# Two Mixtures of Experts on One Core: logits three beats ahead, gates two, and a beat of TensorE in two equal halves

## The reference

```python
router_probs = jax.nn.softmax(x @ router_w + router_b, axis=-1)
top_p, top_i = jax.lax.top_k(router_probs, K)
top_p = top_p / jnp.sum(top_p, axis=-1, keepdims=True)
expert_out = jnp.einsum('bnd,edc->bnec', x, expert_w) + expert_b
gathered = jnp.take_along_axis(expert_out, top_i[..., None], axis=2)
return jnp.einsum('bnk,bnkc->bnc', top_p, gathered)
```

## Time and profile before

| what | value |
|---|---|
| three runs, us | 6378.89, 6384.5, 6384.5 |
| the profiled execution, us | 6384.87 |
| its span, us | 6383.1 |
| mean granted TensorE clock | 0.899 of full speed |
| busy over the span: TensorE, VectorE, ScalarE, POOL | 80%, 68%, 54%, 18% |
| DMA: bytes moved, GB/s over the span | 646.31 MB, 101 |

### The profile page before, as it was taken

How to read it: one execution, slowest core, us unless ns; L and a number is a source line. 1 busy time by engine, 2 the same in 40 slices (tenths; PEclk the granted TensorE clock), 3 DMA queues, 4 the chain that set the end, 5 groups by cost and what they waited for, 6 DMA issues and landing times. The chain is left out here.

```text
span 6383.1 us, 130752 instructions
## 1 busy us (share of the span) xinstructions
PE 5087.2 (80%) x47166; PEld 3307.8 (52%) x47166; DVE 4320.6 (68%) x9480; ACT 3439.0 (54%) x6809; POOL 1148.8 (18%) x1068
## 2 busy tenths in 40 slices
PE   7887887449968885799969997109999999758887
PEld 4664663224523332799969994105555555423332
DVE  7896987696757777522233447697777777568886
ACT  5665665475545664422243226267777767545553
POOL 2332332162200003300000000231121111211110
PEclk9998998759979996799989999559999999878998
DMA  1111113232358884100000235146666666357776
GB/s 36 35 31 35 38 35 92 60 105 90 106 177 275 277 283 141 56 0 0 0 0 0 79 105 146 53 103 77 84 84 84 84 81 81 53 164 236 231 221 213
DMA packets 745076, 646.31 MB, mean 101 GB/s; under 512 B 496551, under 2 KB 578663, under 8 KB 744627
## 3 DMA queue, kind: packets, MB, share of 16 engines
q1 hardware_dynamic: 734387, 634.86, 40.1%
q10 hardware_dynamic: 9216, 4.20, 0.2%
q0 software_dynamic: 1024, 1.05, 0.1%
HBM read 549.78 MB, written 90.20 MB: 100 GB/s over the span
## 5 line engine op out<-in xcount | busy, mean ns | idle before, releaser
L2444 PE MATMUL sw_pC<-sw_row,sw_wc 128*128 128x128 f32 x10160 | 1158.6, 274 | 56.2 <-DVE sw_row L2319 55.0
L2444 PEld LDWEIGHTS sw_pC<-sw_row,sw_wc 128*128 128x128 f32 x10160 | 1147.4, 191 | 58.2 <-DVE sw_row L2319 55.5
L2878 PE MATMUL sp_pC<-sp_work,sp_bands 64*64 64x512 f32 (+11 forms) x14592 | 985.5, 428 | 43.4 <-issue 43.4
L2307 DVE SCALAR_TENSOR_TENSOR sw_row<-sw_pC,sw_y 128x128 f32<-128x128 f32 x1016 | 338.2, 333 | 790.9 <-PE sw_pC L2444 790.9
L2878 PEld LDWEIGHTS sp_pC<-sp_work,sp_bands 64*64 64x64 f32 x14592 | 600.4, 133 | 431.8 <-issue 363.8
L2817 ACT ACTIVATE sp_pC<-sp_pC,sp_par 128x512 f32<-128x512 f32 x832 | 598.4, 741 | 369.3 <-PE sp_pC L2878 346.6
L2015 PE MATMUL t_pO<-t_z,t_ew 128*64 128x512 f32 x2048 | 584.4, 689 | 251.2 <-DVE t_z L1824 235.0
L1824 DVE TENSOR_TENSOR t_z<-t_z,t_ht 128x1024 f32<-128x1024 f32 x512 | 605.1, 1222 | 88.9 <-DMA t_z<-gate_rows 87.4
L2376 ACT ACTIVATE sw_y<-sw_row 128x128 f32 (+1 forms) x762 | 265.9, 349 | 591.8 <-DVE sw_row L2307 591.8
L2774 DVE TENSOR_TENSOR sp_work<-sp_work,sp_pC 128x512 f32<-128x512 f32 x512 | 351.4, 688 | 168.6 <-ACT sp_pC L2817 168.1
L2015 PEld LDWEIGHTS t_pO<-t_z,t_ew 128*64 128x64 f32 x2048 | 132.6, 149 | 553.2 <-issue 267.4
(11 more groups left out here) (385 smaller groups left out, 9576.8 us busy)
## 6 DMA issues: line engine op xcount, KB each, us to landing
t_z<-gate_rows SPq DMA_DIRECT2D x512, 512.0 KB, 6.9
sp_bands<-windows SPq DMA_DIRECT2D x128, 512.0 KB
c_spent<-tokens SPq DMA_DIRECT2D x128, 256.0 KB, 2.6
cb_xs<-tokens SPq DMA_DIRECT2D x128, 256.0 KB, 2.8
wa_xs<-in_x SPq DMA_DIRECT2D x64, 256.0 KB, 2.9
tokens<-wa_xt SPq DMA_DIRECT2D x128, 128.0 KB, 1.9
tokens<-cb_h SPq DMA_DIRECT2D x64, 256.0 KB, 2.7
t_xs<-tokens SPq DMA_DIRECT2D x32, 512.0 KB, 9.5
```

The lines of the kernel that those rows point to most:

```text
L2307: dve.scalar_tensor_tensor(row[par][c][:, :, PAD:PAD + P2], pC[c][:, 0:2 * P2].rearrange("p (b w) -> p b w", b=2), 0.0, line(sweep, c, i), ...
L2444: ins = pe.matmul(pC[c][:, 0:2 * P2], wc[:, sweep, m, :], row[1 - par][c][:, :, m:m + P2], start=(m == 0), stop=(m == 4))
L2878: ins = pe.matmul(out[halves[to], :, low * lo:low * hi], band[halves[k], (NV * g + j) % BANDS, q, AT[k][tap], :], v[halves[k], :, low * at ...
```

## The change

The carried stage gets seven tile buffers instead of six and loads one beat further ahead. The logits are made three beats ahead (TensorE's and ScalarE's m is now n+3) and the gates two (gate, turn_gates and save_gates for n+2). TensorE's beat becomes two halves of like content: mix of a half, turn, add_rest, logits and turn_logits. VectorE's route(n+2) moves from the end of the beat to between the two halves of the first weighing, norm(n+4) to just ahead of it, gate behind the weighing of half 0, stats to the end of the beat and one beat further. ScalarE's root moves to the head of its beat, gap to right behind save_mixed(n, 0), normalise is split over the beat and runs one beat further ahead. A third beat is prepared ahead of the loop.

```diff
--- before.py
+++ after.py
@@ -1571,7 +1571,7 @@
     NB = B * S // (2 * TILE)
     EPS = 1e-5
     BIG = 1e30
-    XR = 6
+    XR = 7
     HR = 3
     with ExitStack() as ctx:
         a = Arena(nc, ctx, stage)
@@ -1657,7 +1657,7 @@
         def x_of(m, i):
 
             if rows is None:
-                return xs[:, m.k, i, :, :]
+                return xs[:, m.n % XR, i, :, :]
             return rows.rearrange("p c b w -> p (b w) c")[:, bass.ds(m.n * J + TS * i, TS), :]
 
         def y_of(m, i):
@@ -1726,8 +1726,8 @@
                     load_columns(2 * n + 11)
                 if n + 1 < NB:
                     spread_gates(n + 1, 0)
-                if rows is None and XR <= n + 4 < NB:
-                    load(n + 4)
+                if rows is None and XR <= n + 5 < NB:
+                    load(n + 5)
                 if n > 0:
                     store(n - 1)
                 if rows is not None and 2 * n + 12 < 2 * NB:
@@ -1821,20 +1821,21 @@
                 dve.wait_ge(ht_saved, 4 * m.n + 2 * i + 2)
                 for q in pairs:
                     dve.wait_ge(g_in[i][q], 16 * m.n + 16)
-                    dve.tensor_tensor(z[:, i, q, :], z[:, i, q, :], ht[:, m.k % HR, i, :], ALU.mult).then_inc(z_ready, 1)
+                    dve.tensor_tensor(z[:, i, q, :], z[:, i, q, :], ht[:, m.n % HR, i, :], ALU.mult).then_inc(z_ready, 1)
 
             def beat(n):
+                later = n.plus(2)
                 weigh(n, 0, [0, 1])
-                if n.plus(1).within(NB):
-                    gate(n.plus(1))
-                weigh(n, 0, [2, 3])
-                if carried is None and n.plus(4).within(NB):
-                    stats(n.plus(4))
-                weigh(n, 1, range(4))
-                if n.plus(2).within(NB):
-                    route(n.plus(2))
                 if carried is None and n.plus(4).within(NB):
                     norm(n.plus(4))
+                if later.within(NB):
+                    route(later)
+                weigh(n, 0, [2, 3])
+                if later.within(NB):
+                    gate(later)
+                weigh(n, 1, range(4))
+                if carried is None and n.plus(5).within(NB):
+                    stats(n.plus(5))
 
             first = Beat(0, 0, 0)
             if carried is None:
@@ -1851,6 +1852,9 @@
             route(first.plus(1))
             if carried is None:
                 norm(first.plus(3))
+            gate(first.plus(1))
+            if carried is None:
+                stats(first.plus(4))
             over_beats(dve, beat)
 
         @block.scalar
@@ -1870,7 +1874,7 @@
                     act.wait_ge(scale_ready, m.n + 1)
                     scale, shift = (v[:, m.k % 2, TS * i:TS * i + TS] for v in (sd, nm))
                 else:
-                    act.wait_ge(x_in[m.k], m.q * 16 + 16)
+                    act.wait_ge(x_in[m.n % XR], 16 * (m.n // XR) + 16)
                     scale, shift = (carried[:, k, J * m.n + TS * i:J * m.n + TS * i + TS] for k in range(2))
                 since(act, h_turned, 4 * m.n + 2 * i - 2)
                 x = x_of(m, i)
@@ -1883,7 +1887,7 @@
                 since(act, z_ready, 8 * m.n - 24 + 4 * i + 4)
                 for s in range(2):
                     act.wait_ge(h_turned, 4 * m.n + 2 * i + s + 1)
-                    act.activation(ht[:, m.k % HR, i, 512 * s:512 * s + 512], pT[s][:, :], ACT.Copy).then_inc(ht_saved, 1)
+                    act.activation(ht[:, m.n % HR, i, 512 * s:512 * s + 512], pT[s][:, :], ACT.Copy).then_inc(ht_saved, 1)
 
             def save_logits(m, i):
                 act.wait_ge(logits_ready, 2 * m.n + i + 1)
@@ -1916,31 +1920,33 @@
                                ACT.Copy).then_inc(y_ready, 1)
 
             def beat(n):
-                m = n.plus(2)
+                m = n.plus(3)
                 due = m.within(NB)
-                ahead = m.plus(1)
-                if n.plus(1).within(NB):
-                    save_gates(n.plus(1))
+                ahead = n.plus(4)
+                later = n.plus(2)
+                if carried is None and ahead.within(NB):
+                    root(ahead)
                 if due:
                     save_turned(m, 0)
                 save_mixed(n, 0)
+                if later.within(NB):
+                    gap(later)
                 if n.n > 0:
                     finish(n.plus(-1), 1)
                 if due:
+                    save_logits(m, 0)
+                if ahead.within(NB):
+                    normalise(ahead, 0)
+                if later.within(NB):
+                    save_gates(later)
+                if due:
                     save_turned(m, 1)
+                save_mixed(n, 1)
                 finish(n, 0)
                 if due:
-                    for i in range(2):
-                        save_logits(m, i)
-                if ahead.within(NB):
-                    normalise(ahead, 0)
-                if carried is None and ahead.plus(1).within(NB):
-                    root(ahead.plus(1))
+                    save_logits(m, 1)
                 if ahead.within(NB):
                     normalise(ahead, 1)
-                if due:
-                    gap(m)
-                save_mixed(n, 1)
 
             def prepare(m, gates_of=None):
                 for i in range(2):
@@ -1960,11 +1966,12 @@
                 root(first.plus(2))
             gap(first)
             prepare(first.plus(1), first)
-            for i in range(2):
-                normalise(first.plus(2), i)
-            gap(first.plus(1))
             if carried is None:
                 root(first.plus(3))
+            gap(first.plus(1))
+            prepare(first.plus(2), first.plus(1))
+            for i in range(2):
+                normalise(first.plus(3), i)
             over_beats(act, beat)
             finish(Beat(NB - 1, (NB - 1) % 6, (NB - 1) // 6), 1)
 
@@ -1977,8 +1984,8 @@
                 pe.wait_ge(h_ready, 2 * m.n + i + 1)
                 for s in range(2):
                     since(pe, ht_saved, 4 * m.n + 2 * i + s - 1)
-                    if i == 0 and s == 0:
-                        since(pe, gs_saved, m.n - 1 if isinstance(m.n, int) and m.n < 2 else m.n)
+                    if s == 0:
+                        since(pe, gs_saved, m.n - 1 if i == 0 or m.n < 3 else m.n)
                     for j in range(4):
                         ins = pe.transpose(pT[s][:, 128 * j:128 * j + 128],
                                            h[:, i, 4 * s + j, :, :].rearrange("p c d -> p (c d)"), ident[:, :])
@@ -1988,7 +1995,7 @@
                 pe.wait_ge(ht_saved, 4 * m.n + 2 * i + 2)
                 since(pe, lg_saved, 2 * m.n + i - 1)
                 for q in range(4):
-                    ins = pe.matmul(pX[i][32 * q:32 * q + 32, 0:256], rw[:, :], ht[:, m.k % HR, i, 256 * q:256 * q + 256],
+                    ins = pe.matmul(pX[i][32 * q:32 * q + 32, 0:256], rw[:, :], ht[:, m.n % HR, i, 256 * q:256 * q + 256],
                                     start=True, stop=True)
                 ins.then_inc(logits_ready, 1)
 
@@ -2005,11 +2012,11 @@
                 pe.transpose(pT[0][:, 0:128], gates[:, m.k % 2, :, :].rearrange("p e j -> p (e j)"),
                              ident[:, :]).then_inc(gates_turned, 1)
 
-            def mix(m, i, pairs, gates_of=None):
+            def mix(m, i, gates_of=None):
                 since(pe, oc_saved, 2 * m.n + i - 1)
-                for q in pairs:
+                for q in range(4):
                     if gates_of and q == 2:
-                        turn_gates(gates_of, 4 * m.n + 7)
+                        turn_gates(gates_of, min(4 * m.n + 13, 4 * NB))
                     pe.wait_ge(z_ready, 8 * m.n + 4 * i + q + 1)
                     for s in range(2):
                         ins = pe.matmul(pO[i][64 * s:64 * s + 64, :], ew[:, q, :], z[:, i, q, 512 * s:512 * s + 512],
@@ -2036,28 +2043,28 @@
                     turn_logits(m, i)
 
             def beat(n):
-                m = n.plus(2)
+                m = n.plus(3)
                 due = m.within(NB)
-                mix(n, 0, range(4), n.plus(1) if n.plus(1).within(NB) else None)
+                mix(n, 0)
                 if due:
                     turn(m, 0)
                 if n.n > 0:
                     add_rest(n.plus(-1), 1)
                 if due:
+                    logits(m, 0)
+                    turn_logits(m, 0)
+                mix(n, 1, n.plus(2) if n.plus(2).within(NB) else None)
+                if due:
                     turn(m, 1)
                 add_rest(n, 0)
                 if due:
-                    for i in range(2):
-                        logits(m, i)
-                mix(n, 1, [0])
-                if due:
-                    for i in range(2):
-                        turn_logits(m, i)
-                mix(n, 1, [1, 2, 3])
+                    logits(m, 1)
+                    turn_logits(m, 1)
 
             first = Beat(0, 0, 0)
             prepare(first)
```

(1 more changed line is left out.)

## The result

The changed kernel takes 6679.64 us (median of four runs, 6674.02 to 6683.52) against 6384.5: the ratio is 1.0462, with a 95% interval of 1.0444 to 1.048. The forecast was 6620, its range 6515 to 6700. The profiled execution took 6678.73 us.

A forecast was written before the change was run, and what follows sets the result against it. No engine is full; a loop of waits from route to route sets the beat. Added were 61 us (carried), 107 (image), 2 (small terms) and 70 (clock): 240 on 6384.9, 6625, rounded to 6620; range 6515 to 6700.

The forecast's parts named there:

- The loop: Carried stage: turn_logits, route, two pairs, both mixes and TensorE's rest close a loop, 21.1 us a beat against 18.98, 61 more.
- The clock: TensorE at half clock after idling inside the mix: 1.0 us a carried beat, 1.5 an image beat, 70 us in all.
- The image stage's sum: Image stage: same loop with longer terms and norm's wait, 26.7 us a beat against 22.78, 107 us more.
- The place of norm in the loop: Image stage: norm ahead of route waits for ScalarE's root behind normalise, adding 3.8 us to 27 beats.
- the rival in which ScalarE comes to root early: Image stage: norm doesn't hold route, 29 beats of 23.3 us, 15 more instead of 107; 6523 us, chance 0.09.
- The small terms: Gates, store, seventh tile's load and third prepared beat: +2 us together, between -10 and +15.
- Saves it at the end: Preparing a third beat costs TensorE and ScalarE a beat's work ahead of the loop, saved at its end; within +2 us.
- Hidden costs: VectorE's wait for z goes but gives nothing back; route(2) keeps about its old time; seventh tile's load 1.9 us.
- The clock stays up: Rival: TensorE pays nothing for its clock, 61 + 107 + 2 us more, 6555 us; chance 0.16.
- no change: Rival: the new order is as long as the old, no change that shows; chance 0.03.
- Every beat pays: Rival: every beat pays TensorE's clock fully, 1.7 us carried and 2.5 image, 117 in all; 6672 us, chance 0.12.
- Faster: Rival: route finds its logits ready, beats fall to 16.1 us (DMA, carried) and 18.7 (VectorE, image); 6183 us, chance 0.08.

The follow-up runs named there:

- the run with the repeated products: Changed kernel, with TensorE mixing pairs 0 and 1 of half 0 once more (carried) or three times more (image) ahead of the real mix: 6605.5 us, ratio 1.0349.

## Why the prediction was right, and by how much its terms were off

**The loop.** That the order closes a loop, through which engines it runs and that it is longer than the old one, is what the traces show. In the carried beat above, four of six terms are the forecast's to 0.03: route 3.95, two pairs 2.35 (2.34), turn and add_rest 2.77, logits and their turning 1.53 (1.5). The two others are longer by 0.74 (1.87 instead of 1.13) and 0.69 (10.09 instead of 9.4), and both hold instructions at half clock (the two pairs, and turn at 1.97 instead of 1.09). With the clock up, 21.1 was forecast and 21.1 measured, in the run with the repeated products and in the two beats of the changed kernel itself.

**The clock** was under-sized in the carried stage: 1.0 us a beat on record, 1.5 measured, since 27 of the 29 beats have a half-clock stretch, where before about one of two had, and eight of them have two. In the image stage 1.5 was forecast and 1.5 came. The upper bound, 1.7 and 2.5 us a beat, was not reached in the mean, but the eight beats with two stretches paid 2.2 to 2.3.
The Trainium skill ("TensorE: Matmul & The Clock Gate", section "HAM oscillation") has as its rule that each burst behind a long enough wait starts throttled again. The trace agrees in 27 of 29 carried beats, with a clock of 0.50 behind 3.35 us of idle time. The idle time alone does not decide: behind 3.36 us at 1880.96 the clock stayed up, and in the kernel before the 2.59 us ahead of 2106.12 left it up (eight instructions in 2.12 us), while those ahead of 2125.00 did not (3.58).

**The image stage's sum** was 26.7 and 27.0 is measured with the clock nearly up, with two errors that nearly cancel: route was put at 5.0 and took 4.1, because POOL's addition no longer falls on it, and the four pairs of half 1 were put at 4.68 and took 6.08 in the beat shown, 5.7 in the mean, because it falls on them (the addition itself is 2.49 us long there instead of 1.6). That the sum of the two came out right is luck. The forecast saw the long route in the earlier trace rows and did not ask what made it long; in the kernel before, that beat shows it:

```profile
5940.33 1.63 POOL L1756 TENSOR_TENSOR passes<-passes,t_xs 128x512 f32<-128x512 f32 x1 [9.81 <-DMA t_xs<-tokens]
5940.48 1.63 DVE L1793 TENSOR_TENSOR t_eq<-t_lg,t_mx 128x128 f32<-128x128 f32 x1
```

The place of norm in the loop was right: 3.74 against 3.8, and the rival in which ScalarE comes to root early is out.

**The small terms** are the step that failed most against its size: +2 on record, bounds -10 to +15, and 22.6 measured. "Saves it at the end" was wrong. route(n+2) stands in the middle of the first weighing now instead of the end of the beat. When the last route starts, TensorE still has six halves to mix (both of that beat and four more), before it had four and three pairs of a fifth: 1.25 halves more. One half in the last beats lasts from 6634.04 to 6639.41 + 1.07, 6.4 us, which makes 8.0 of the 12.4 us in the image stage. The carried stage's half has a shorter add_rest (1.12 and 1.05 beside the mix's 3.65), 5.5 us with the overlap, which makes 6.9 of the 7.5 us that lie between that stage's last route and TensorE's last add_rest (44.4 after 36.9). The other 2.0 of its 9.5 lie behind that, up to the image stage's route(2). The rest, idle time behind route among it, was not separated. A sum from route to route does not see this.

**Hidden costs** were as forecast: VectorE's wait for z went and gave nothing back, route(2) came 0.3 us later, and nothing shows the seventh tile's load.

**The whole:** 104.8 against 61 + 29, 166.5 against 107 + 41, 22.6 against 2. The sum is 293.9 instead of 240. All three errors have the same sign. The time lies above the band that the forecast held likeliest, 6580 to 6655, and inside the range by 20 us, because the range's upper end was worked out with the clock's full price, which was not paid; that this covers the small terms too is luck.

**The rivals.** "The clock stays up" and "no change" are out. "Every beat pays" comes nearest in its total, 6672, for part of the reason that it gave: every beat pays, but less than its price, and the tails make up the rest. "Faster" described what happens if the loop is open, 16.1 and 18.7 us a beat and 6183 us. It did not happen, but when route was moved and the store spread, it did: 16.2 and 19.3 us a beat, 6212.65 us. The 18.7 rests on VectorE, which is busy 97% there. The 16.1 was worked out from the DMA engines, and TensorE's own order sets the beat; that the two lie so near to each other is luck.

What is left open: how much of the image stage's 27.0 is clock that the repeated products did not restore (its granted clock was 0.96), and why the clock falls behind one idle time and not behind an equal one.

## What to carry to other kernels

When no engine is full, follow one beat's chain from a wait back to itself and add up its terms from the rows: here the forecast's sums met the measured carried beat to 0.1 us, before the change (19.03 for 18.98) and, with the clock up, after it (21.1 for 21.1). Making something a beat further ahead did not open this loop; it opened when the instruction that waits was moved behind enough ready work of its neighbour. And what was moved off one instruction, a wait or a contending addition, fell mostly on the next one that was there, so ask of each long instruction what made it long.

## What the runs showed of the hardware that was not expected

TensorE's granted clock fell after an idle time of 3.35 us in 27 of 29 carried beats, and stayed up in 28 of 29 when the idle time was cut to 1.64 by 1.9 us of products that nobody needs; with those of the image stage, 74 us less in all. VectorE's small products of 0.29 us took up to 1.60 beside a POOL addition of 1.60, and four large ones 6.08 instead of 4.6, while that addition was stretched to 2.49. In the first case POOL had begun 0.14 us earlier, in the second VectorE 0.25 us earlier: the later one waited. The DMA engines held a share of 0.98 at 327 GB/s over 430 us without any wait for z that is worth naming (3.9 us in all).
